# A two-layer gated FFN kernel: the second layer's shared part as one expert of 704 with stationary weights

## What is computed

```python
xf = x.reshape(-1, DIM)                        # 2048 rows of 512
y = _moe(xf, gate_w, w1, w2, w3)               # 32 experts of 352, 6 for each row
shared = jax.nn.silu(xf @ sw1) * (xf @ sw3) @ sw2    # sw1, sw3: 512 x 704; sw2: 704 x 512
return (y + shared).reshape(shape)
```

## Time and profile before

| | |
|---|---|
| median of 3 runs | 1536.73 us (1535.74 to 1540.0) |
| profiled execution, its own time | 1533.35 us |
| its span in the profile | 1531.5 us |
| mean granted TensorE clock | 0.954 |
| PE busy | 1301.7 us, 85% |
| VectorE (DVE) busy | 1083.8 us, 71% |
| ScalarE (ACT) busy | 767.2 us, 50% |
| GpSimd (POOL) busy | 630.6 us, 41% |

### The profile page before, as it was taken

One profiled execution on the slowest core, in us unless ns is written; L12 is line 12 of the kernel. 1 busy time (PEld: TensorE's weight loads), 2 busy tenths in 40 slices (PEclk: granted clock), 3 DMA queues, 4 the chain that ended last, 5 costly groups with the idle time before them and its releaser, 6 DMA issues.

```text
span 1531.5 us, 25913 instructions
## 1 busy us (share of the span) xinstructions
PE 1301.7 (85%) x9004; PEld 874.4 (57%) x9004; DVE 1083.8 (71%) x2186; ACT 767.2 (50%) x1436; POOL 630.6 (41%) x478
## 2 busy tenths in 40 slices
PE   0045664689999499989899999999999999999997
PEld 0023342244444265656577777777777777777775
DVE  8999988888989558888745556555655565656532
ACT  3466664645555444442155555555555555555432
POOL 2244533443443244430134454554545445544532
PEclk9987766999999699999999999999999999999999
DMA  3556645778997666651348999999999999999764
GB/s 105 173 159 198 159 117 120 149 170 182 240 229 177 188 196 192 175 162 51 132 123 189 218 211 224 224 201 225 222 195 217 205 223 237 216 225 213 128 111 54
DMA packets 240030, 273.19 MB, mean 178 GB/s; under 512 B 164448, under 2 KB 164576, under 8 KB 239776
## 3 DMA queue, kind: packets, MB, share of 16 engines
q1 hardware_dynamic: 203248, 179.51, 48.5%
q0 software_dynamic: 36656, 92.03, 30.6%
HBM read 167.87 MB, written 70.32 MB: 156 GB/s over the span
## 4 chain that ended last, share of the span: by engine, by line
PE 70%; DVE 22%; issue 5%; ACT 2%; POOL 0%; DMA 0%; POOLq 0%; SPq 0%; DVEq 0%; ACTq 0%
PE psO L2090 22%; PE psG L2019 22%; PE psG L1986 10%; DVE FX L1488 6%; PE psH L2019 5%; PE psG L2025 3%; DVE FX L1470 2%; DVE FX L1463 2%; PE psX L1947 2%; DVE FX L1459 2%; DVE FX L1495 1%; DVE FX L1473 1%; DVE FX L1480 1%; DVE H L1805 1%; PE psX L1885 1%
## 5 line engine op out<-in xcount | busy, mean ns | idle before, releaser
L1167 POOL DMA_INDIRECT out<-OB,posb x128 | 227.8, 1779 | 337.9 <-ACT OB L1396 184.8
L1986 PE MATMUL psG<-Whi,XSp 128*128 128x352 f16 (+2 forms) x952 | 258.4, 362 | 9.5 <-issue 9.3
L2090 PE MATMUL psO<-Whi,RT 128*128 128x512 f16 x768 | 249.8, 380 | 2.2 <-DVE RT L1796 1.9
L2019 PE MATMUL psG<-XSp,Whi 128*128 128x256 f16 x1024 | 170.9, 273 | 1.1 <-ACT XSp L1331 1.1
L2019 PE MATMUL psG<-KW,Whi 128*128 128x256 f16 x1024 | 170.9, 273 | 0.0
L1778 DVE SCALAR_TENSOR_TENSOR RT<-RT,psG 128x256 f32<-128x256 f32 (+1 forms) x154 | 64.6, 420 | 135.2 <-ACT RT L1366 135.2
L1986 PEld LDWEIGHTS psG<-Whi,XSp 128*128 128x128 f16 x952 | 97.3, 102 | 101.6 <-issue 33.4
L1986 PE MATMUL psG<-Wlo,XSp 128*128 128x352 f16 (+2 forms) x476 | 151.1, 362 | 0.0
L1149 POOL DMA_INDIRECT XG<-xrows,posb x96 | 99.8, 1040 | 112.4 <-DVE posb L1680 54.4
L2090 PE MATMUL psO<-Wlo,RT 128*128 128x512 f16 x384 | 145.5, 379 | 0.0
L1396 ACT ACTIVATE OB<-psO,WSL 128x512 f32<-128x512 f32 x128 | 87.4, 683 | 113.6 <-PE psO L2090 113.6
(11 more groups left out here) (263 smaller groups left out, 2850.3 us busy)
## 6 DMA issues: line engine op xcount, KB each, us to landing
FX<-W SPq DMA_DIRECT2D x66, 544.0 KB, 7.1
ST<-W SPq DMA_DIRECT2D x64, 544.0 KB, 5.6
ST<-W SPq DMA_DIRECT2D x23, 512.0 KB, 4.0
slots<-OB SPq DMA_DIRECT2D x39, 256.0 KB, 3.4
KW<-fT SPq DMA_DIRECT2D x32, 256.0 KB, 3.7
xrows<-XG SPq DMA_DIRECT2D x20, 256.0 KB, 2.8
y0rows<-x SPq DMA_DIRECT2D x8, 512.0 KB, 5.2
y0rows<-OB POOLq DMA_DIRECT2D x16, 256.0 KB, 4.7
```

The source lines that it names most:

```text
L1167: G.indirect_dma_start(out=Y1[:, :], out_offset=bass.IndirectOffsetOnAxis(ap=idx[1][:, j:j + 1], axis=0), in_=OB[o % 4][:, :], in_offset=N ...
L1986: op = M.matmul(o, hx[:, x, q * P:q * P + P], w(half_, off + c, nn), start=first, stop=last)
L2019: op = M.matmul(sums(half_ * 256), W[:, to:to + P], x(which, q), start=(q == 0 and which == 0 and W is Whi), stop=(q == 3 and W is Wlo))
L2090: op = M.matmul(psO[bank(o)][:, :], h(x, q), w(half_, off0 + q * 512), start=(q == 0 and x == 0 and half_ is Whi and first), stop=(q == NK ...
```

## The change

The two halves of the shared expert become one expert of 704 inner columns, cut in thirds of 256, 256 and 192. Gate and up products are made by new branches of `f_gu` with the weights stationary: 48, 48 and 36 matmuls of 128 columns for a tile, numbered t = 0 to 47 (`THIRDS` = 48), and the routed thirds are numbered from 48 on. The 192 gate and 192 up columns of the last third fill three groups of 128 (gate 512 to 639; gate 640 to 703 beside up 640 to 703; up 512 to 639), and the low half of the last 64 inner rows is moved on to the partitions 64 to 127 of the high half (`f_move`), so that the down product of a tile is 17 matmuls of 512 columns instead of 18. The float32 activation goes through the two tiles H32 in turn, the split one through two buffers FT, the second of which lies where the last piece (50) of a routed expert's weights went; that piece is now converted at the start of the routed part. Down products of a tile are issued together, in the slots with odd b.

```diff
-WIDE = RING.index(51)
+WIDE = RING.index(50)
...
-    def shared(b, what):
-
-        if 0 <= b < 32:
-            yield what, S1 + b
+    def parts(b):
+
+        t = 3 * (b // 2)
+        if b < 0:
+            return
+        if b % 2 == 0:
+            if b:
+                yield "f_split", t - 1
+            yield "f_gu", t
+        else:
+            yield "f_gu", t + 1
+            if b >= 3:
+                yield "f_move", t - 1
+            yield "f_split", t
+            yield "f_gu", t + 2
+            yield "f_split", t + 1
+
+    def shared_down(b):
+
+        if b % 2 == 1 and b >= 3:
+            yield "down", S1 + b - 2
...
-            yield from shared(b, "gu_pe")
-            if b >= 0:
-                yield from shared(b - 1, "h_turn")
-            yield from shared(b, "gu")
+            yield from parts(b)
...
-                yield from shared(b - 2, "down")
+                yield from shared_down(b)
...
-        yield from loads(2, 51)
+        yield from loads(2, 50)
 
     yield "r_place", 3
-    yield from loads(5, 56)
+    yield from loads(5, 55)
...
+    yield "f_split", THIRDS - 2
+    yield "down", R1 - 3
+    yield "f_split", THIRDS - 1
+    yield "f_move", THIRDS - 1
+    yield "down", R1 - 1
...
     yield "clear", 0
+    yield from splits(1)
...
+        FT = [(HSall[:, 0:768], HSall[:, 768:1536]), (Whi[:, 17280:18048], Wlo[:, 17280:18048])]
...
+            if k == 50:
+                return R1 - 1
...
             def f_gu(t):
-                p, c = divmod(t, 3)
+                p, c = divmod(t - THIRDS, 3)
                 rows = 96 if c == 2 else P
                 eng.wait_ge(b_fgu, t + 1)
-                if t == 0:
+                if p < 0:
+                    if t >= 2:
+                        eng.wait_ge(b_flo, t - 1)
+                    else:
+                        eng.wait_ge(b_ht, S1)
+                    A.activation(H32[t % 2][:, 0:256], f_psum(t)[:, 0:256], ACT.Tanh,
+                                 scale=0.5 * UN).then_inc(b_ftanh, 1)
+                    return
...
+            def f_move(t):
+                hi, lo = FT[t // 3 % 2]
+                eng.wait_ge(b_flo, t + 1)
+                A.copy(hi[64:128, 640:768], lo[0:64, 640:768]).then_inc(b_fmove, 1)
+
             def f_split(t):
...
+                if p < 0:
+                    eng.wait_ge(b_down, S1 + 2 * max(t // 3 - 1, 0))
+                    A.copy(FT[t // 3 % 2][0][:, c * 256:c * 256 + 256], H32[t % 2][:, 0:256]).then_inc(b_fhi, 1)
+                    return
...
+                if p < 0:
+                    H = H32[t % 2][:, 0:256]
+                    V.scalar_tensor_tensor(out=H, in0=H, scalar=1.0, in1=ps[:, 0:256], op0=ALU.add,
+                                           op1=ALU.mult).then_inc(b_fsil, 1)
+                    eng.wait_ge(b_fsil, t + 1)
+                    if c == 2:
+                        V.scalar_tensor_tensor(out=H[0:64, 128:256], in0=H[0:64, 128:256], scalar=gain,
+                                               in1=ps[64:128, 128:256], op0=ALU.mult, op1=ALU.mult)
+                    w = 128 if c == 2 else 256
+                    V.scalar_tensor_tensor(out=H[:, 0:w], in0=H[:, 0:w], scalar=gain, in1=ps[:, 256:256 + w],
+                                           op0=ALU.mult, op1=ALU.mult).then_inc(b_fh, 1)
+                    return
...
+                if p < 0:
+                    (hi, lo), at = FT[t // 3 % 2], c * 256
+                    V.tensor_tensor(lo[:, at:at + 256], H32[t % 2][:, 0:256], hi[:, at:at + 256],
+                                    ALU.subtract).then_inc(b_flo, 1)
+                    return
...
+                if t >= 5:
+                    eng.wait_ge(b_fh, t - 4)
+                if p < 0:
+                    z, ps, wide = S1 + t // 3, f_psum(t), 384 if c == 2 else 512
...
+                    for k in range(wide // P):
+                        for q in range(4):
+                            to = 18432 + 2048 * c + q * wide + k * P
+                            for which, W in ((0, Whi), (1, Whi), (0, Wlo)):
+                                op = M.matmul(ps[:, k * P:k * P + P], W[:, to:to + P],
+                                              XSp[ring(z)][:, which, q * P:q * P + P],
+                                              start=(q == 0 and which == 0 and W is Whi), stop=(q == 3 and W is Wlo))
+                    op.then_inc(b_fgu, 1)
+                    return
...
+                elif what == "shared":
+                    eng.wait_ge(b_fmove, j // 2 + 1)
...
+                if what == "shared" and l == 1:
+                    for k in range(6):
+                        to = 18432 + 5632 + k * 512
+                        for x, half_ in ((0, Whi), (0, Wlo)) + (((1, Whi),) if k < 5 else ()):
+                            op = M.matmul(psO[bank(o)][:, :], FT[j // 2 % 2][x][:, k * P:k * P + P],
+                                          half_[:, to:to + 512], start=(k == 0 and x == 0 and half_ is Whi),
+                                          stop=(k == 5 and half_ is Wlo))
+                    op.then_inc(b_down, 2)
+                    return
```

More of the change, by code:

```diff
@@ L144, in loads @@
             k = RING[done["load"]] if done["load"] < len(RING) else len(PIECES)
-            if k < upto and done["load"] < sum(j < done["lo"] for j in RING) + (2 if k < 51 else 5):
+            if k < upto and done["load"] < sum(j < done["lo"] for j in RING) + (2 if k < 50 else 5):
                 yield "w_load", k
@@ L551, in stages @@
     yield "hot", 22
-    yield from shared(31, "gu_pe")
-    yield from shared(30, "h_turn")
+    yield "f_gu", THIRDS - 2
+    yield "f_move", THIRDS - 4
     yield "hot_pe", 21
+    yield "f_split", THIRDS - 3
     yield "hot", 23
     yield "hot_pe", 22
+    yield "f_gu", THIRDS - 1
     yield "hot_pe", 23
@@ L581, in tile_in @@
         if 0 <= t < 3 * PAIRS:
-            yield what, t
+            yield what, THIRDS + t
     yield "gather", R1 + 3
     yield "clear", 0
+    yield from splits(1)
     for n in (R1, R1 + 1):
@@ L609, in stages @@
         if p < PAIRS:
-            yield "f_split", 3 * p
+            yield "f_split", THIRDS + 3 * p
         yield from turn(n + 4, True)
@@ L614, in stages @@
         if p < PAIRS:
-            yield "f_split", 3 * p + 1
+            yield "f_split", THIRDS + 3 * p + 1
         yield from pair_weights(p)
@@ L1399, in _ @@
                         f_hi=f_hi_, f_turn=f_turn, r_top=r_top, w_hi=w_hi_, turn=turn, gu=gu, h_turn=h_turn,
-                        f_gu=f_gu, f_split=f_split, h_low=h_low, down=down)
+                        f_gu=f_gu, f_split=f_split, f_move=f_move, h_low=h_low, down=down)
             for what, n in stages():
@@ L2058, in down @@
                 o, first, last = finished(n)
-                if n < R1:
+                if l == 0:
                     eng.wait_ge(b_hslo, n + 1)
+                elif what == "shared":
+                    eng.wait_ge(b_fmove, j // 2 + 1)
+                    if j == 1:
+                        eng.wait_ge(*low(34))
+                    first = True
                 else:
-                    eng.wait_ge(b_flo, 3 * (j // 2) + 3)
+                    eng.wait_ge(b_flo, THIRDS + 3 * (j // 2) + 3)
                 if first:
@@ L2138 @@
               np.concatenate([f["L0_ffn_w_down"], f["L0_ffn_sw_down"][None]]), 2)
-    def halves(a):
-        return a.reshape(512, 2, 352).transpose(1, 0, 2)
-    W1 = pack(np.concatenate([f["L1_ffn_w1"], halves(f["L1_ffn_sw1"])]),
-              np.concatenate([f["L1_ffn_w3"], halves(f["L1_ffn_sw3"])]),
-              np.concatenate([f["L1_ffn_w2"], f["L1_ffn_sw2"].reshape(2, 352, 512)]), 3)
+    W1 = np.concatenate([pack(f["L1_ffn_w1"], f["L1_ffn_w3"], f["L1_ffn_w2"], 3), np.zeros((2, 128, 4352), np.float32)])
+    both = np.concatenate([f["L1_ffn_sw1"], f["L1_ffn_sw3"]], axis=1).reshape(4, 128, 1408).transpose(1, 0, 2)
+    cuts = [np.concatenate([np.arange(a, a + 256), np.arange(704 + a, 960 + a)]) for a in (0, 256)]
+    cuts.append(np.concatenate([np.arange(512, 704), np.arange(1344, 1408), np.arange(1216, 1344)]))
+    last = f["L1_ffn_sw2"].reshape(704, 512)
+    downs = [last[k * 128:k * 128 + 128] for k in range(5)] + [np.concatenate([last[640:], last[640:]])]
+    W1[32:34] = np.concatenate([both[:, :, c].reshape(128, -1) for c in cuts] + downs, axis=1).reshape(
+        128, 2, 4352).transpose(1, 0, 2)
     order = np.concatenate([np.arange(352), np.arange(672, 704), np.arange(352, 608)])
```

52 lines of the change are left out of this document (24 added, 28 removed).

## The result

The changed kernel takes 1561.2 us (median of four runs, 1560.2 to 1566.3), the kernel before beside it 1536.2: a ratio of 1.0178 with a 95% interval of 1.0158 to 1.0198. It is slower by 25 us where 9.4 were forecast, and outside the range of 1532 to 1555. The profiled execution took 1560.52 us (span 1558.7), 27.2 more than that of before.

What follows compares the result with a forecast made beforehand. TensorE was taken to bound up to 585 us and from 720, VectorE's queue between. Terms +10.3 there, -1.0 ahead, -1.7 behind and +1.8 at the routed start gave +9.4, a median of 1546 us; range 1532 to 1555.

Steps and rivals of the forecast that it cites:

- TensorE per tile: Gate, up and down matmuls of a tile: 11.05 us in place of 11.70, a saving of 0.65 a tile.
- rival 3: Clock falls to its lower level in longer pauses ahead of `f_turn` and at the routed start: +6, 1552 us; 7%.
- VectorE's queue sets the pace: From 585 to 720 us, 8.5 tiles: VectorE bounds and TensorE's work is hidden; sum of the stretch +10.3 us.
- extra +4.7: 585 to 720 us: VectorE's added operations, 0.55 us a tile over 8.5 tiles, have no cover.
- Hand-over, +4.0: 585 to 720 us: tanh of t + 2 waits for VectorE's low half, 0.45 us in each of nine odd slots.
- Waiting for the long down products, +1.6: 585 to 720 us: VectorE waits some 0.4 us for a tile's down products, in four steps.
- Exclusion, +1.0: 585 to 720 us: VectorE's low halves and GpSimd's SBUF reads exclude each other; +1.0 us, between 0 and 4.2.
- Ahead of the long stretch, -1.0: 520 to 585 us: TensorE saves 2.9, the half-clock first block 1.6, even slots cost 3.5; together -1.0 us.
- Even slots without down products, +3.5: s = 1 to 5: nothing covers the way from last gate and up matmul to L1544; about 0.7 us, five times.
- Start of the routed part, +1.8: Behind the last down product: ScalarE converts piece 50 ahead of the copy L1331, which comes 1.8 us later.
- Behind the long stretch, -1.7: 720 to 763 us: three tiles save 2.0 us, of which a wait for `r_red` takes 0.3.
- The relief of -1.0: 585 to 720 us: no down product between `r_pos` and logits at s = 13, light half in slot 23; -1.0 us.

Runs made afterwards that it cites:

- three tiles: Changed kernel with three tiles for the float32 activation instead of two, so tanh needn't wait for the low half: 1561.0 us, 1.0155.
- the two small runs: Changed kernel with low halves on 8 columns: 1558.0 us, 1.0134; kernel before with one more VectorE operation a half: 1539.4 us, 1.0011.
- filler: Changed kernel with unused 512-column matmuls put ahead of TensorE's waits at eight places: 1561.3 us, 1.0153.

## Why the forecast was wrong in size

The premise that failed is the one under the whole sum: that one engine sets the pace of each stretch, TensorE up to 585 us and VectorE from there to 720, so that its added work counts one for one and the other's costs nothing. The sum so put at nothing the slower clock, and in s = 1 to 5 also VectorE's added work and the exclusion. By place, it missed 5.2 us in s = 1 to 5 (+4.2 for -1.0), 6.6 in s = 6 to 15 (+16.9 for +10.3), 1.8 behind them (+0.1 for -1.7) and 2.5 at the start of the routed part (+4.3 for +1.8).

**TensorE per tile: right in kind.** 56 ns a matmul and 3.67 us for down hold. The saving in the stage is 8.8 us by the account above, where 10.4 + 1.6 = 12.0 were forecast. The Trainium skill, page "TensorE: Matmul & The Clock Gate", section "Back-to-back issue gap", has about 81 ns for such a stream; 48 in 2.68 us is against it.

**The clock: left out of the sum,** and given 7% as rival 3, half hidden. The idle pieces of 2.8 to 4.7 us brought TensorE to its lower level (1.2 GHz) behind most of them, 0.93 of full clock for 0.98 in the stage. TensorE's work took 11.3 us longer by the account, an estimate that rests on one profile; what that cost the stage was 1.4 us alone and 4.8 with three tiles. The mechanism was rival 3's. That the pauses grew because TensorE's work got shorter fits the chain, but no run shows it by itself.

**"VectorE's queue sets the pace": failed.** It was read from one unbroken row of work and from the earlier trace rows. VectorE's busy share fell from 87% to 82% in the steps where it should have risen, and with 35 us less of work in the stage the change gained 12, not 21. The extra +4.7 priced at one for one is worth 0.2 to 0.3 for one by the two small runs.

**Hand-over, +4.0: at most 1.7 alone.** Its wait was there, and with the wait gone VectorE waited for down products.

**Waiting for the long down products, +1.6: mis-sized.** VectorE's waits at that line went from 4.6 to 15.5 us. I had compared two sums of durations in one step and counted four steps; it is eleven waits, since TensorE comes late to them too, behind its own wait and at half clock. How much of the 10.9 is path isn't shown: splitting or shifting the products gained nothing.

**Exclusion, +1.0: 2.3,** within its bounds, by the two stages, but the place was wrong. It adds some 4 us in s = 1 to 5 (4.8 off the change, 0.8 off the kernel before), where the forecast had none, and nothing in s = 6 to 15 (3.2 and 4.9), where it had the +1.0. That the total lies within the bounds is luck.

**Ahead of the long stretch, -1.0: it was +4.2.** Saving and half-clock term assumed TensorE as the bound there. Its busy time did fall, 58.5 to 56.7 us, with the clock at 0.89 for 0.95, but its idle time grew from 2.5 to 8.5. Without GpSimd's reads the steps take 60.4 us, and with VectorE's shared work away 61.4. **Even slots without down products, +3.5:** not confirmed; splitting them gave nothing for the whole, and whether it is part of these 4.2 is open.

**Start of the routed part, +1.8:** the wait was 2.3; the 2.0 of clock on top were left out, though the forecast named the place in rival 3.

**Behind the long stretch, -1.7: it was +0.1.** TensorE's busy time fell by 2.1 us there, 43.7 to 41.5, at full clock, and the time didn't follow. The relief of -1.0 isn't seen by itself.

What remains open: with the clock kept, the wait for tanh gone and the exclusion away, the change still has 18 us more of TensorE without work in the stage (36.9 against 18.9), of which the saving gives back 8.8. About half of it is VectorE's amount: with that work away TensorE's idle time is 28.8 us (250.71 - 221.88) for 37.6. That the rest is the order in which three in-order queues meet is argued, not shown. It fits the runs, since moves of one item cost up to 55 us, but no order tried removed it, and VectorE's reduced work wasn't run together with a kept clock.

## What to carry to other kernels

Where two engines are each busy 85 to 90% and hand work to and fro every step, neither is the bound, and a change that shortens one and lengthens the other can lose twice: the pauses grow on the first, and its clock falls in them. Compare the same steps before and after, not the same microseconds: a fixed window hides in which steps the time went. Price the clock in the main sum wherever a pause grows beyond what the trace shows as harmless. A hand-written order fits the block sizes it was written for; when they change from 24 equal matmuls to 48 and 84, look at every step's first and second slot before counting a saving.

## What the runs showed that I hadn't expected

Two reliefs of 0 to 4 us each (filler, 1.0153; three tiles, 1.0155) gave 1.0096 together. Leaving out GpSimd's reads gave the kernel before 4.6 us already (1531.1 against 1535.6 beside it; 3.4 by the ratio), with only 16 pieces of 2.1 us. And 84 matmuls of 128 columns kept 56 ns each with a new load for every one, so the change's premise on TensorE was sound, while the time was lost elsewhere.
